# Remainders of a three-part bf16 split formed by TensorE instead of VectorE

## The reference

```python
xbc = u @ W_x.T
dt_low, B_ssm, C_ssm = jnp.split(xbc, [DT_RANK, DT_RANK + D_STATE], axis=-1)
dt = clip(softplus(dt_low @ W_dt.T + b_dt) + DT_MIN, DT_MIN, DT_MAX)
def step(h, inp):                       # for each token, h: 512 x 16
    dA = jnp.exp(dt_t[:, :, None] * A)
    h = dA * h + (dt_t * u_t)[:, :, None] * B_t[:, None, :]
    y = jnp.einsum('bdn,bn->bd', h, C_t)
y = (y + u * D_param) * silu(z)
return y @ W_out.T + residual
```

## Time and profile before

| what | value |
|---|---|
| median of 3 runs | 4129.58 us |
| profiled execution | 4124.94 us, its span 4123.2 us |
| VectorE busy over the span | 3554.3 us, 86% |
| TensorE matmul busy | 3309.6 us, 80% |
| GpSimd busy | 2624.9 us, 64% |
| ScalarE busy | 2318.6 us, 56% |
| mean granted TensorE clock | 0.894 |

### The profile page before, as it was taken

How to read it: one execution, slowest core, us unless ns; L and a number is a source line. 1 busy time by engine, 2 the same in 40 slices (tenths; PEclk the granted TensorE clock), 3 DMA queues, 4 the chain that set the end, 5 groups by cost and what they waited for, 6 DMA issues and landing times. The chain is left out here.

```text
span 4123.2 us, 61159 instructions
## 1 busy us (share of the span) xinstructions
PE 3309.6 (80%) x21708; PEld 1525.3 (37%) x21708; DVE 3554.3 (86%) x5837; ACT 2318.6 (56%) x4294; POOL 2624.9 (64%) x2459
## 2 busy tenths in 40 slices
PE   5979999999993999999667777777777777776467
PEld 3633333333332555555322222222222222222166
DVE  5768888888854999999369999999999999999966
ACT  5626666666672344444366666666666666666422
POOL 1102322323231888888369999999999999998723
PEclk8969999999997999999887888888888888887689
DMA  4894565555613111110112122211222222221132
GB/s 145 281 186 65 77 81 80 83 84 75 87 32 87 34 44 45 44 48 30 33 47 64 60 69 65 64 54 53 69 66 63 64 69 61 67 57 52 41 95 85
DMA packets 274957, 299.58 MB, mean 73 GB/s; under 512 B 35583, under 2 KB 205686, under 8 KB 274646
## 3 DMA queue, kind: packets, MB, share of 16 engines
q1 hardware_dynamic: 274654, 295.68, 31.1%
HBM read 210.22 MB, written 84.51 MB: 71 GB/s over the span
## 5 line engine op out<-in xcount | busy, mean ns | idle before, releaser
L1719 POOL TENSOR_TENSOR d_dBu<-d_dtu,d_Bn 128x1024 f32<-128x1024 f32 x512 | 1218.2, 2413 | 0.1
L1560 ACT ACTIVATE d_dA<-d_dt,d_decay 128x512 f32<-128x512 f32 x1024 | 691.4, 687 | 411.0 <-DVE d_h L1802 409.0
L750 ACT ACTIVATE b_P<-b_pT 128x512 f32<-128x512 f32 (+1 forms) x1120 | 570.3, 576 | 310.3 <-PE b_pT L656 307.4
L1802 DVE TENSOR_TENSOR_SCAN d_h<-d_dA,d_last_h,d_dBu 128x512 f32<-128x512 f32 x512 | 616.3, 1261 | 16.3 <-ACT d_dA L1560 11.0
L1802 DVE TENSOR_TENSOR_SCAN d_h<-d_dA,d_dBu 128x512 f32<-128x512 f32 x512 | 585.7, 1200 | 37.5 <-ACT d_dA L1560 36.5
L783 DVE CUSTOM_DVE_ANT_0 b_pS<-b_pS,mask_qk 128x512 f32<-128x512 f32 (+1 forms) x768 | 501.2, 686 | 57.9 <-PE b_pS L666 52.7
L628 POOL TENSOR_SCALAR_AFFINE_SELECT b_P<-b_P 128x128 f32<-128x128 f32 (+2 forms) x608 | 192.7, 321 | 525.6 <-ACT b_P L750 513.8
L666 PE MATMUL b_pS<-KS,QS 99*128 99x512 bf16 (+3 forms) x1536 | 474.9, 339 | 33.4 <-PEq L85 21.7
L656 PE MATMUL b_pT<-QS,KS 118*128 118x512 bf16 (+3 forms) x1536 | 448.9, 329 | 3.1 <-ACT b_P L750 2.1
L1809 DVE TENSOR_TENSOR d_h<-d_h,d_C 128x2048 f32<-128x2048 f32 x192 | 433.4, 2257 | 0.7 <-PE d_C L1444 0.7
L1444 PE MATMUL d_C<-d_bc,d_pick 96*128 96x512 bf16 x256 | 116.1, 453 | 387.2 <-DVE d_h L1809 387.0
(11 more groups left out here) (313 smaller groups left out, 5981.3 us busy)
## 6 DMA issues: line engine op xcount, KB each, us to landing
d_Bn<-scratch_bs SPq DMA_DIRECT2D x128, 512.0 KB, 4.9
scratch_parts<-a_part SPq DMA_DIRECT2D x48, 512.0 KB, 4.1
QS<-scratch_parts SPq DMA_DIRECT2D x192, 128.0 KB, 7.3
KS<-scratch_parts SPq DMA_DIRECT2D x192, 128.0 KB, 7.7
scratch_v<-a_v SPq DMA_DIRECT2D x16, 1024.0 KB, 7.6
V<-scratch_v SPq DMA_DIRECT2D x32, 512.0 KB, 11.5
a_x<-in_L_attn_x_dram SPq DMA_DIRECT2D x16, 512.0 KB, 7.7
scratch_o<-b_O SPq DMA_DIRECT2D x16, 512.0 KB, 9.6
```

Of the source, the lines that this page charges most:

```text
L750: act.activation(t[:, heads[0]:heads[-1] + 1, c * CH:c * CH + w], pT[:, place % RING, 0:len(heads) * w].rearrange("p (h w) -> p h w", w=w) ...
L1560: act.activation(dA[:, m % 2, :], dt[:, c.k % 2, m, :], ACT.Exp, scale=decay[:, m, n:n + 1]).then_inc(dA_d, 1)
L1719: pool.tensor_tensor(product(c, n)[:, 2 * j:2 * j + 2, :], dtu[:, c.k % 2, 2 * j:2 * j + 2, :], Bn[:, n // BG % 2, n % BG, :].unsqueeze(1) ...
L1802: dve.tensor_tensor_scan(h[:, n % HS, m, :], dA[:, m % 2, :], product(c, n)[:, m, :], start, ALU.mult, ALU.add).then_inc(scanned, 1)
```

## The change

TensorE forms the remainders in PSUM: first xb times a piece of the identity (f32), then the parts already made, with weights -1 (bf16), added onto it. ScalarE reads the result and rounds it to bf16 into its place in `bc`. The bank gets two more uses, R1 and R2, between DT and GT. VectorE's two subtractions, the buffers rest and mid and four semaphores go. The later uses of the bank move by half a slot, and some normalisations and readings of ScalarE change their slots.

```diff
-        TR, IN, CV, WX, DT, GT = 0, KD, KD + MD, KD + 2 * MD, KD + 2 * MD + 1, KD + 3 * MD + 1
+        TR, IN, CV, WX, DT, R1, R2, GT = 0, KD, KD + MD, KD + 2 * MD, KD + 2 * MD + 1, KD + 3 * MD + 1, KD + 3 * MD + 2, KD + 3 * MD + 3
-        xb, rest = sb("xb", [96, CH]), sb("rest", [96, CH])
-        mid = sb("mid", [96, CH], BF16)
+        xb, neg = sb("xb", [96, CH]), sb("neg", [96, 2, 32], BF16)
 # TensorE
                 if n == 0:
-                    wait(pe, lo_d, c.times(1, 1))
-                    wait(pe, mid_put, c.times(1, 1))
+                    wait(pe, act_read, c.times(NF, R2 + 1))
 # output(e, j)
-                    wait(pe, act_read, e.times(NF, 2 * NF + (GT if j else CV + MD)))
+                    wait(pe, act_read, e.times(NF, 2 * NF + (R2 if j else CV + MD)))
 # bank(q, i)
-                if i == GT:
+                if i == R2:
                     wait(pe, ag_d, q.times(2, -2))
+            def remainder(q, i):
+                wait(pe, hi_d, q.times(1, 1))
+                p = bank(q, i)[DR:96, :]
+                pe.matmul(p, K["ident"][0:96, DR:96], xb[:, :], start=True, stop=False)
+                pe.matmul(p, neg[:, i - R1, :], bc[:, q.k % 2, :], start=False, stop=True).then_inc(front_mm, 1)
             run(pe, spread,
                 ({6: lambda e: output(e, 0)},
-                 {2: lambda q: convolve(q, 0), 3: lambda q: convolve(q, 1), 4: lambda q: convolve(q, 2), 5: lambda q: convolve(q, 3),
-                  8: lambda q: project_dt(q, 0), 9: lambda q: project_dt(q, 2), 12: lambda q: project(q, GT, MD), 13: lambda q: project(q, GT + 2, MD + 2)},
-                 {14: lambda f: turn(f, 0), 15: lambda f: project(f, IN, 0)}),
+                 {0: lambda q: project(q, IN + 1, 1), 2: lambda q: convolve(q, 0), 3: lambda q: convolve(q, 1), 4: lambda q: convolve(q, 2), 5: lambda q: convolve(q, 3),
+                  8: lambda q: project_dt(q, 0), 9: lambda q: project_dt(q, 2), 10: lambda q: remainder(q, R1), 12: lambda q: remainder(q, R2),
+                  13: lambda q: project(q, GT + 1, MD + 1), 14: lambda q: project(q, GT + 3, MD + 3)},
+                 {15: lambda f: turn(f, 1)}),
                 sums,
                 ({10: lambda e: output(e, 1)},
                  {0: lambda q: project(q, IN + 2, 2), 1: lambda q: project(q, IN + 3, 3), 7: project_x, 8: lambda q: project_dt(q, 1), 9: lambda q: project_dt(q, 3),
-                  12: lambda q: project(q, GT + 1, MD + 1), 13: lambda q: project(q, GT + 3, MD + 3)},
-                 {14: lambda f: turn(f, 1), 15: lambda f: project(f, IN + 1, 1)}))
+                  12: lambda q: project(q, GT, MD), 13: lambda q: project(q, GT + 2, MD + 2)},
+                 {14: lambda f: turn(f, 0), 15: lambda f: project(f, IN, 0)}))
 # ScalarE
             def take_x(q):
-                wait(act, lo_d, q.times(1, 0))
             def split_mid(q):
-                wait(act, rest_d, q.times(1, 1))
-                act.activation(mid[DR:96, :], rest[DR:96, :], ACT.Copy).then_inc(mid_d, 1)
-                wait(act, mid_d, q.times(1, 1))
-                act.activation(bc[32:DR, q.k % 2, :], mid[DR:96, :], ACT.Copy).then_inc(mid_put, 1)
+                act.activation(bc[32:DR, q.k % 2, :], bank(q, R1)[DR:96, :], ACT.Copy).then_inc(act_read, 1)
+            def split_lo(q):
+                act.activation(bc[0:32, q.k % 2, :], bank(q, R2)[DR:96, :], ACT.Copy).then_inc(act_read, 1)
             run(act, first_two,
                 ({0: last_gate},
-                 {0: lambda q: inner(q, 1), 1: lambda q: inner(q, 2), 2: lambda q: inner(q, 3), 8: take_x, 9: lambda q: below(q, 1), 10: lambda q: below(q, 3), 11: step_size,
-                  13: lambda q: gate(q, 1), 14: lambda q: gate(q, 3)},
-                 {4: lambda f: normalise(f, 0, (2, 3)), 11: lambda f: normalise(f, 1, (1,)), 12: lambda f: normalise(f, 1, (3,)), 15: lambda f: turned(f, 1)}),
+                 {0: lambda q: inner(q, 0), 1: lambda q: inner(q, 2), 2: lambda q: inner(q, 3), 8: take_x, 9: lambda q: below(q, 1), 10: lambda q: below(q, 3), 11: step_size,
+                  13: lambda q: gate(q, 0), 14: lambda q: gate(q, 2)},
+                 {4: lambda f: normalise(f, 0, (2, 3)), 11: lambda f: normalise(f, 1, (0,)), 12: lambda f: normalise(f, 1, (3,)), 15: lambda f: turned(f, 0)}),
                 last_two,
                 ({},
-                 {2: lambda q: convolved(q, 0), 3: lambda q: convolved(q, 1),
+                 {0: lambda q: inner(q, 1), 2: lambda q: convolved(q, 0), 3: lambda q: convolved(q, 1),
                   4: lambda q: convolved(q, 2), 5: lambda q: convolved(q, 3), 6: silu, 8: lambda q: (below(q, 0), split_hi(q)), 9: lambda q: below(q, 2),
-                  10: grow, 11: split_mid, 12: lambda q: gate(q, 0), 13: lambda q: gate(q, 2)},
-                 {3: lambda f: normalise(f, 0, (0, 1)), 10: lambda f: normalise(f, 1, (0,)), 11: lambda f: normalise(f, 1, (2,)),
-                  14: lambda f: turned(f, 0), 15: lambda f: inner(f, 0)}))
+                  10: lambda q: (split_mid(q), grow(q)), 12: split_lo, 13: lambda q: gate(q, 1), 14: lambda q: gate(q, 3)},
+                 {3: lambda f: normalise(f, 0, (0, 1)), 11: lambda f: normalise(f, 1, (1, 2)), 15: lambda f: turned(f, 1)}))
 # VectorE, set-up
+            dve.memset(bc[:, :, :], 0.0).then_inc(const, 1)
+            for i in range(2):
+                dve.tensor_scalar(neg[:, i, :], K["ident_bf"][0:96, DR:96], -1.0, None, ALU.mult).then_inc(neg_set, 1)
+            dve.wait_ge(neg_set, 2)
+            dve.tensor_scalar(neg[32:DR, 1, :], K["ident_bf"][32:DR, 32:DR], -1.0, None, ALU.mult).then_inc(const, 1)
 # VectorE
-            def split_rest(q):
...
-                dve.tensor_tensor(rest[rows, :], xb[rows, :], bc[rows, q.k % 2, :], ALU.subtract).then_inc(rest_d, 1)
-            def split_lo(q):
...
-                dve.tensor_tensor(bc[0:32, q.k % 2, :], rest[rows, :], mid[rows, :], ALU.subtract).then_inc(lo_d, 1)
             run(dve, scan, weigh_before,
                 ({1: gate_y, 6: lambda e: gate_out(e, 0), 11: lambda e: gate_out(e, 1)},
-                 {9: split_rest, 12: split_lo},
+                 {},
```

More of the change, by code:

```diff
@@ L1316, in state_space @@
         y, dA, pC, pf = ps("y", [P, NQB, CH]), ps("dA", [P, 2, CH]), ps("C", [P, CH]), ps("f", [P, CH])
-        w_in, const, set_up, x_in, e_in, m_in = sem("w_in"), sem("const"), sem("set_up"), sem("x_in"), sem("e_in"), [sem("m_in0"), sem("m_in1")]
+        w_in, const, neg_set, set_up, x_in, e_in, m_in = sem("w_in"), sem("const"), sem("neg_set"), sem("set_up"), sem("x_in"), sem("e_in"), [sem("m_in0"), sem("m_in1")]
         g_in = [sem("g_in0"), sem("g_in1")]
@@ L1322, in state_space @@
         front_mm, act_read, carried, silu_u, silu_z = (sem(n) for n in ("front_mm", "act_read", "carried", "silu_u", "silu_z"))
-        hi_d, rest_d, mid_d, lo_d, mid_put = (sem(n) for n in ("hi", "rest", "mid", "lo", "mid_put"))
+        hi_d = sem("hi")
         exp_d, dt_d, dtu_d = (sem(n) for n in ("exp", "dt", "dtu"))
@@ L1779, in _ @@
             dve.wait_ge(w_in, 16 * 7)
-            dve.wait_ge(const, 10 + NQB)
+            dve.wait_ge(const, 12 + NQB)
             dve.tensor_scalar(b_dt[:, :, :], b_dt[:, :, :], -1.0, V_MAX, ALU.mult, ALU.add).then_inc(const, 1)
@@ L1785, in _ @@
                     dve.tensor_scalar(cdiag[:, m, j, :], K["ident"][:, :], conv_w[:, m, j:j + 1], None, ALU.mult).then_inc(const, 1)
-            dve.wait_ge(const, 11 + NQB + MD * (1 + TAPS))
+            dve.wait_ge(const, 13 + NQB + MD * (1 + TAPS))
             dve.tensor_scalar(decay[:, :, :], decay[:, :, :], -1.0, None, ALU.mult).then_inc(set_up, 1)
@@ L1841, in carry @@
                     dve.tensor_copy(xi[:, :, 0:TAPS - 1], xi[:, :, CH:CH + TAPS - 1]).then_inc(carried, 1)
-            def split_rest(q):
[L1844 to L1847, removed]
-                dve.tensor_tensor(rest[rows, :], xb[rows, :], bc[rows, q.k % 2, :], ALU.subtract).then_inc(rest_d, 1)
-            def split_lo(q):
-                rows = slice(DR, 96)
-                wait(dve, mid_d, q.times(1, 1))
-                wait(dve, rest_d, q.times(1, 1))
-                dve.tensor_tensor(bc[0:32, q.k % 2, :], rest[rows, :], mid[rows, :], ALU.subtract).then_inc(lo_d, 1)
             def gate_y(e):
```

## The result

The changed kernel takes 4172.65 us (median of 4 runs, 4161.72 to 4196.67) against 4128.76 us; the ratio is 1.0114, 95% interval 1.0096 to 1.0133. It is slower; 4101 was predicted. The profiled execution has a span of 4172.0 us, 48.8 more than before. In the whole document ratios leave out three single slow executions (4185.84, 12522.67 and 6442.40 us, one each of the runs with the thrown-away matmul, with R2 in slot 10 and with the thrown-away matmul among the two moves), while a median in us counts every execution.

The account below looks back on a forecast made before the run. The state-space stage was taken to run at VectorE's pace (98% busy). Slots 9 to 13 were to give 31.3 us, less 2.7 for the fill: 28.6 off the median 4129.58, so 4101.0 us, range 4095 to 4108.

Parts of the forecast that it names:

- the 28.6: Total forecast gain in us: 31.3 from slots 9 to 13 of all chunks, less 2.7 before the first scan.
- the fill: Time before the first scan: R1, R2 and their readings enter ScalarE's ping-pong with TensorE; 2.7 us more, bounds 0 to 6.
- rival D: Around slot 11's weighing, step input and finish, GpSimd holds VectorE; slots 12 and 13 give nothing: 4117 us, chance 0.06.
- those 0.44 us go with the remainder: GpSimd's products beside the second subtraction took 5.11 us, the next pair 4.67; this excess was to vanish with the subtraction.
- In later slots the same readings stand with the same spacing: Slots after 13: moved projections and readings cost nothing; one slow pair, up to 1.8 us, if ScalarE's cover were gone.
- rival B: Slot 13: the first projection takes 3.75 instead of 1.98 us, so the slot gives -0.75; 4128 us, chance 0.14.
- rival C: Slots 10 and 13: TensorE stays at 1.2 GHz through R1, R2, sum and first projection; 4153 us, chance 0.09.
- First remainder: Slots 9 to 11: removing VectorE's first subtraction gains 1.2 us per even chunk and 0.85 per odd chunk.
- Second remainder: Slots 12 and 13: removing VectorE's second subtraction, 1.48 us even or 1.24 odd, gains 1.05 us per chunk.
- Waits added: TensorE's output 1 in slot 10 waits for the R1 reading, R2 for VectorE's gate-out; put at nothing.

Follow-up runs that it names:

- the thrown-away matmul: Changed kernel with one unused f32 matmul of 512 columns ahead of TensorE's wait for VectorE's gate of y in slot 2: 4144.76 us, ratio 1.0040.
- R2 in slot 10: Changed kernel with R2 late in slot 10 behind R1, no half-slot shift, and the carry copy on ScalarE: 4126.42 us, ratio 0.9991.
- the thrown-away matmul among the two moves: Changed kernel, carry copy on ScalarE, modulation on GpSimd, slot 2 order as the change left it, plus the unused matmul in slot 2: 4097.69 us, ratio 0.9923.
- the two moves: Carry copy moved to ScalarE and modulation to GpSimd: kernel before 4107.71 us, ratio 0.9949; changed kernel 4098.30 us, ratio 0.9928.
- the shift alone: Kernel before with gate projections, transposes and inner projections half a slot later, without R1 and R2, subtractions kept: 4140.63 us, ratio 1.0028.
- the mended order: Changed kernel with TensorE's first sum of slot 2 issued behind convolution 0: 4126.45 us; with copy on ScalarE and modulation on GpSimd too, 4073.85 us.

## Why the prediction was wrong

Where it looked, the sum was somewhat high. For the fourteen chunks of the table it comes to 7 x (2.25 + 1.90) = 29 us in slots 9 to 13, and the table gives 24 (with slot 13 of odd chunks, the copy's, left out). The 33.9 us above are no confirmation of the 28.6: they hold the 10.4 us of the subtraction's longer wait. The loss lies elsewhere. In the profiled execution slot 2 cost 34 us more, the carry copy and the modulation 28.6 + 5.1 = 34, the fill 6; less the 24 that is 50, and the span grew by 48.8. The prediction failed in two steps.

**1. Instructions left out of the account: the carry copy and the modulation.** In this step a term was put at nothing without a reason. The prediction used the shared port only to make rival D less likely, and said of GpSimd's delay "those 0.44 us go with the remainder". The two instructions that stayed on VectorE with such operands were not priced. By ratios, moving both takes 1.0114 - 0.9928 = 0.0186, 77 us, off the changed kernel and 0.0051, 21 us, off the kernel before, 56 us more. Not all of the 56 is their own time. The two lines were 37.2 us of VectorE's busy time in the stage before (24.2 + 13.0) and 70.9 after, 34 more; with the moves slot 2 of even chunks also went back from 8.99 to 6.65, another 16 us; and in the kernel before the moves made the first subtraction 10.4 us longer, which hides a part of their gain there. What they cost the changed kernel by themselves is so 34 us more than before in the execution profiled, and its runs differ in that number.

**2. "In later slots the same readings stand with the same spacing ... I cost it at nothing."** ScalarE's readings did; the place of TensorE's slow clock did not. In the even chunk shown the granted clock of the first sum was 1.00 before and 0.50 after, and the reading of convolution 0, on which the decays of slot 3 wait, came late. The runs confirm the place (the shift alone, and the mended order). What moves the slow level there is not shown: it isn't the idle time ahead, since sums behind 3.03 to 3.15 us of it ran at full clock in several kernels. The prediction weighed the slow clock as rivals B and C, but in slots 10 to 13. Slot 2 cost 2.3 x 7 + 2.5 x 7 = 34 us in the profiled execution; mending the order with the copy and the modulation moved gave 23, half of it in slot 4.

Point by point, from the changed kernel's trace:

- First remainder: even slots 9 to 11 together 22.21 us against 23.23, a gain of 1.0 (forecast 1.2); odd 0.7 (0.85). R1 took 1.02 + 0.38 = 1.4 us, as taken. TensorE's rows of slots 10 and 12:

```profile
2414.89 1.02 PE L1537 MATMUL d_f<-d_xb,ident 96*32 96x512 f32 x2 [0.55 <-ACT d_dt L1672]
2415.75 0.38 PE L1538 MATMUL d_f<-d_bc,d_neg 96*32 96x512 bf16 x1
...
2428.43 1.89 PE L1537 MATMUL d_f<-d_xb,ident 96*32 96x512 f32 x2
2430.11 0.63 PE L1538 MATMUL d_f<-d_bc,d_neg 96*32 96x512 bf16 x1
2430.68 2.01 PE L1459 MATMUL d_y<-d_h,d_eye 32*32 32x512 f32 x32
2432.62 2.37 PE L1514 MATMUL d_f<-d_xnT,w_inT 128*128 128x512 f32 x4
```

- Second remainder: R2 took 1.89 + 0.63 = 2.5 us, as taken; the sum behind it 2.01 instead of 1.17, the first projection 2.37 instead of 2.0 us. Slots 12 and 13 of even chunks gave 0.44 us, not 1.05. The sum's 0.84 is what rival C put on it; of rival B's 1.8 for the projection 0.4 came.
- Fill: the first scan came at 2112.03 instead of 2106.32, 5.7 us later; forecast 2.7, bound 6. In the other runs with R1 and R2 it came between 2107.9 and 2116.6, so one execution doesn't price the fill.
- Waits added: none of them stands among the waits of scans shown above.
- Rival D: no wait for GpSimd's products is among the waits above; GpSimd held VectorE in another way, through the port.

The Trainium skill ("SBUF — State Buffer", Who interferes with whom) says that a copy in a two-port mode, or an instruction with two SBUF inputs against a GpSimd instruction that reads SBUF, excludes the other and that the later one waits. The traces agree for most waits: the copies of 2.6 us and the first subtractions end with, or 0.55 us after, one instruction of GpSimd. They differ in the longest waits: 14.18 us over six instructions of GpSimd, not one.

Open: what decides whether VectorE gets the port at GpSimd's next boundary or only when GpSimd stops; what decides where TensorE's slow level falls, and why it falls in slot 2 of odd chunks alone once the copy and the modulation are moved.

## What to carry to other kernels

Before taking an instruction off the busiest engine, list every other instruction of it that shares the SBUF port with GpSimd, and give each as its upper bound the length of GpSimd's unbroken run there, not its mean. Move such instructions first (here 21 us by itself), then make the change; the same split change was +44 us with them, -9 us without them (4098.30 against 4107.71), and -34 us with the first sum moved as well. When work is moved on TensorE, compare the granted clock slot by slot, and put matmuls that another engine waits for ahead of those that themselves wait.

## What the runs showed that was not expected

- A VectorE copy of 12 elements per partition took 14.2 us beside an unbroken run of GpSimd, and 0.17 us in the fill, without one.
- A modulation of 1.23 us alone took 6.5 to 7.2 us in the same way; with the copy on ScalarE it was hit more often (six of its seven executions in even chunks in the kernel with R2 in slot 10, none in the kernel before).
- With the same 3.03 us of idle ahead, the first sum took 2.02 us in one chunk and 1.15 in another of the same kernel.
